# Attention's products in halves of 64 rows, two side by side, with the low part of a pair made one pair later

## The reference

```python
# layer 0: x = x + out_proj(layernorm(selective scans of conv(in_proj(layernorm(x)))) * silu(z))
# layer 1, with O = 96 and N = 4096 positions an image
g_x, theta_x, phi_x = (_conv1x1(x, w, b).reshape(B, O, N) for w, b in ...)
f1 = jnp.einsum('bon,bom->bnm', theta_x, phi_x)
f_div_C = jax.nn.softmax(f1, axis=-1)
y = jnp.einsum('bnm,bom->bon', f_div_C, g_x)
return _conv1x1(y, W_w, W_b) + x
```

## Time and profile before

| what | value |
|---|---|
| median of 3 runs | 9250.66 us (9244.29 to 9259.2) |
| profiled execution | 9256.15 us |
| its span, first to last instruction | 9254.4 us |
| mean granted TensorE clock | 0.981 |
| busy: TensorE, VectorE, ScalarE, GpSimd | 93%, 80%, 66%, 36% |

### The profile page before, as it was taken

One profiled execution on the slowest core, in us unless ns is written; L12 is line 12 of the kernel. 1 busy time (PEld: TensorE's weight loads), 2 busy tenths in 40 slices (PEclk: granted clock), 3 DMA queues, 4 the chain that ended last, 5 costly groups with the idle time before them and its releaser, 6 DMA issues. The chain is left out here.

```text
span 9254.4 us, 103902 instructions
## 1 busy us (share of the span) xinstructions
PE 8642.6 (93%) x26448; PEld 4648.4 (50%) x26448; DVE 7377.0 (80%) x8229; ACT 6091.9 (66%) x7440; POOL 3295.4 (36%) x1853
## 2 busy tenths in 40 slices
PE   7899998999989998899988999889998899988999
PEld 3336743367433674336733367333673336733476
DVE  6987779877798777987679876798767987689876
ACT  6765677656776567765677556775567755677566
POOL 2870028600286002860038600385003850038400
PEclk9999999999999999999999999999999999999999
DMA  1320013200132001320013200232002320023200
GB/s 53 111 87 13 10 56 112 80 13 10 57 111 82 11 11 59 115 76 10 11 63 111 76 10 11 65 116 71 8 12 68 111 73 8 11 72 114 66 8 12
DMA packets 286693, 503.21 MB, mean 54 GB/s; under 512 B 142155, under 2 KB 143215, under 8 KB 253431
## 3 DMA queue, kind: packets, MB, share of 16 engines
q1 hardware_dynamic: 286199, 497.81, 17.9%
HBM read 467.99 MB, written 29.47 MB: 54 GB/s over the span
## 5 line engine op out<-in xcount | busy, mean ns | idle before, releaser
L1400 DVE TENSOR_TENSOR pl<-pf,ph 128x1024 fp32r<-128x1024 f32 x1024 | 1254.3, 1225 | 1007.1 <-ACT ph L1020 999.5
L1253 DVE TENSOR_TENSOR_SCAN h<-ps,h,dbu 128x512 f32<-128x512 f32 x1536 | 1884.2, 1267 | 59.8 <-POOL dbu L1087 29.9
L1087 POOL TENSOR_TENSOR dbu<-bs,du 128x1024 f32<-128x1024 f32 x768 | 1808.1, 2369 | 54.1 <-POOL du L1078 54.1
L1020 ACT ACTIVATE ph<-pf 128x1024 fp32r<-128x1024 f32 x1024 | 1085.3, 1060 | 750.3 <-PE ps L708 750.0
L885 ACT ACTIVATE ps<-dt,negA 128x512 f32<-128x512 f32 x1536 | 1037.5, 687 | 684.8 <-DVE h L1253 684.8
L1014 ACT ACTIVATE pf<-ps 128x1024 f32<-128x1024 f32 x1024 | 1050.4, 1026 | 530.7 <-PE ps L695 513.3
L1066 POOL MEMSET pad<- 128x66 f32 (+1 forms) x64 | 7.2, 200 | 3853.2 <-DVE fa L1429 3853.0
L1384 DVE TENSOR_REDUCE mx<-ps 128x1 f32<-128x512 f32 x1792 | 1168.6, 683 | 78.8 <-PE ps L606 62.5
L1261 DVE TENSOR_TENSOR hc<-h,ps 128x1024 f32<-128x1024 f32 x768 | 937.9, 1221 | 110.3 <-PE ps L487 19.7
L487 PE MATMUL ps<-xhl,selr 128*128 128x512 f32 x1536 | 768.1, 585 | 238.8 <-DVE hc L1261 238.6
L1072 POOL TENSOR_TENSOR dt<-dt,ze 128x1024 f32<-128x1024 f32 x256 | 604.0, 2359 | 1061.3 <-ACT dt L878 1061.3
(11 more groups left out here) (204 smaller groups left out, 14540.6 us busy)
## 6 DMA issues: line engine op xcount, KB each, us to landing
bs<-rows SPq DMA_DIRECT2D x256, 1024.0 KB, 5.1
bs<-rows SPq DMA_DIRECT2D x512, 256.0 KB, 6.1
xa<-in_x SPq DMA_DIRECT2D x130, 256.0 KB, 2.9
xb<-in_x SPq DMA_DIRECT2D x130, 128.0 KB, 3.0
out<-fa SPq DMA_DIRECT2D x64, 256.0 KB, 2.1
rdb<-rden SPq DMA_DIRECT2D x56, 192.0 KB, 3.4
out<-fa SPq DMA_DIRECT2D x64, 128.0 KB, 2.4
xhl<-ct SPq DMA_DIRECT2D x256, 8.0 KB
```

Of the source, the lines that this page charges most:

```text
L1020: A(ph[:, mp % 2, :, :], pf[:, mp % 2, :, :], ACT.Copy).then_inc(S["ph_ready"], 1)
L1087: pool.tensor_tensor(dbu[:, q, :, :], bs[par][:, q, :, :], du[:, r:r + 1, :].to_broadcast([P, 2, T]), ALU.mult).then_inc(S["dbu_ready"], 1)
L1253: dve.tensor_tensor_scan(h[:, j, ::step], ps[:, 2 + e, ::step], dbu[:, q, e, ::step], h[:, j, end:end + 1], ALU.mult, ALU.add)\
L1400: TT(pl[:, mp % 2, :, :], pf[:, mp % 2, :, :], ph[:, mp % 2, :, :].bitcast(F32), ALU.subtract)\
```

## The change

Every fp32r product of attention is cut into halves over rows 0 to 63 and 64 to 127 of the array, issued in turn, so that neighbours in the queue use different halves and different banks. The 96 channels of scores, three times, and the shift row are laid out anew over 64 + 64 + 64 + 64 + 33 rows for each of a pair's blocks, in `th1`, `thx`, `thy` for the queries and `ph1`, `ph2`, `ph3` for the keys. `scores_1` makes three halves for either block and `scores_2` two more. `weigh` gathers the upper halves in bank 5, so the old sum now is two banks that are read and added (`read_sum` on both ScalarE and VectorE). A block of maxima is a lower half ahead of three pairs of halves and an upper half behind them, in one bank (6 or 7). `TOPS`, `WY_AT` and `WR_AT` move. VectorE makes the low part of a pair in the next pair's turn, between its second and third block. The low part of theta is made in four pieces, the high part gets a second copy, and phi's rows are copied to their other places in the mixing steps. The shift goes to two rows with one DMA each. The diff, cut (where code of `top`, `scores` and `weigh` is removed, it is that above):

```diff
-        thc = [[sb(f"thc{q}{i}", [O + 1, T], F32R, where=vx) for i in range(2)] for q in range(2)]
+        th1 = [sb(f"th1{q}", [P, T], F32R, where=vx) for q in range(2)]
+        thx = [sb(f"thx{q}", [P, T], F32R, where=vx) for q in range(2)]
+        thy = [sb("thy0", [P, T], F32R, where=vx)]
         mx = sb("mx", [P, 4, NU // 4], where=vx)
...
-        TOPS = [0] + [2] * 4 + [3] * 8 + [0] * 3
+        TOPS = [0] * 2 + [2] + [3] * 10 + [0] * 3
         FIRST_TOP = [sum(TOPS[:m]) for m in range(MP)]
         assert sum(TOPS) == NU
         LAG = 2
-        DEN_AT, RB_AT, WY_AT, WR_AT = 5, 8, 10, 12
+        DEN_AT, RB_AT, WY_AT, WR_AT = 5, 8, 13, 15
+        LOW, UP = slice(0, R), slice(R, P)
...
                         sp.wait_ge(S["nmx_ready"], i + 2)
-                        for t in range(4):
-                            sp.dma_start(thc[1 - par][0][O:O + 1, t * P:(t + 1) * P].bitcast(F32), nmr[:, t:t + 1].bitcast(F32))\
-                                .then_inc(S["shift_loaded"], 16)
+                        for row in (thx[1 - par][LO:LO + 1, :], thy[1 - par][O:O + 1, :]):
+                            sp.dma_start(row.bitcast(F32).rearrange("o (p j) -> o p j", j=4), nmr[:, :].bitcast(F32)).then_inc(S["shift_loaded"], 16)
...
-                def top(j, i, par, t, m, bank):
...
+                def top(j, i, c, par, rows):
+                    n = b * (NU * (NCH - 1)) + c * NU + (j + 1)
+                    t, m = j // (NU // 4), j % (NU // 4)
+                    if rows == LOW:
+                        if j == 0:
+                            pe.wait_ge(S["thh_ready"], i + 1)
+                            pe.wait_ge(S["thl_ready"], i * 4 + 1)
+                        pe.wait_ge(S["top_read"], i * NU + (j + 1))
+                    else:
+                        pe.wait_ge(S["top_half"], n)
+                    q = mm(ps[:, 6 + j % 2, :], th1[par][rows, :].rearrange("p (k t) -> p t k", t=4)[:, t, :], ph1[rows, m * T:(m + 1) * T],
+                           start=(rows == LOW), stop=(rows == UP))
+                    q.then_inc(S["top_half" if rows == LOW else "top_ready"], 1)
...
-                def scores(mp, c, i, par, first):
+                def scores_1(mp, c, i, par, first, j=None):
                     s = i * MP + mp
...
+                    if mp == 0 and not first:
+                        pe.wait_ge(S["thl_ready"], i * 4 + 4)
+                        pe.wait_ge(S["thx_ready"], i + 1)
+                        pe.wait_ge(S["shift_loaded"], b * (32 * (NCH - 1)) + (c * 32 + 32))
+                    pe.wait_ge(S["pf_ready"], s + 1)
+                    bank = 2 * (mp % 2)
+                    one, other = slice(2 * mp * P, (2 * mp + 1) * P), slice((2 * mp + 1) * P, (2 * mp + 2) * P)
+                    t1, tx = th1[par], thx[par]
+                    def low(n):
+                        if n < 2:
+                            return mm(ps[:, bank, :], (ph1, ph2)[n][LOW, one], t1[LOW, :], start=(n == 0), stop=False)
+                        return scores_0(mp, par, 0)
+                    def up(n):
+                        if n < 2:
+                            return mm(ps[:, bank + 1, :], (ph1, ph2)[n][UP, other], (t1, tx)[n][UP, :], start=(n == 0), stop=False)
+                        return scores_0(mp, par, 1)
+                    if j is not None:
+                        top(j, i + 1, c, 1 - par, LOW)
+                    for n in range(2 if mp == 0 and first else 3):
+                        if j is None:
+                            low(n)
+                            q = up(n)
+                        else:
+                            up(n)
+                            q = low(n)
+                    q.then_inc(S["s1_done"], 1)
+                    if j is not None:
+                        top(j, i + 1, c, 1 - par, UP)
+                def scores_0(mp, par, e, stop=False):
+                    rows = (slice(0, LO + 1), slice(R, O + 1))[e]
+                    return mm(ps[:, 2 * (mp % 2) + e, :], ph3[rows, mp * P:(mp + 1) * P], (thx, thy)[e][par][rows, :], start=False, stop=stop)
+                def scores_2(mp, i, par, first):
+                    pe.wait_ge(S["s1_done"], i * MP + (mp + 1))
+                    bank = 2 * (mp % 2)
+                    one, other = slice(2 * mp * P, (2 * mp + 1) * P), slice((2 * mp + 1) * P, (2 * mp + 2) * P)
+                    t1, tx = th1[par], thx[par]
                     early = mp == 0 and first
...
+                    mm(ps[:, bank, :], ph1[UP, one], t1[UP, :], start=False, stop=False)
+                    mm(ps[:, bank + 1, :], ph1[LOW, other], t1[LOW, :], start=False, stop=False)
+                    mm(ps[:, bank, :], ph2[UP, one], tx[UP, :], start=False, stop=not early)
+                    q = mm(ps[:, bank + 1, :], ph2[LOW, other], t1[LOW, :], start=False, stop=not early)
                     if early:
...
+                        q.then_inc(S["s2_done"], 1)
                         shift(i)
+                        pe.wait_ge(S["s2_done"], b + 1)
                         pe.wait_ge(S["thc_ready"], b + 1)
...
+                        scores_0(mp, par, 0, True)
+                        q = scores_0(mp, par, 1, True)
                     q.then_inc(S["st_ready"], 1)
-                def weigh(mp, i):
+                def weigh(mp, e, i, c, par=0, j=None):
                     s = i * MP + mp
...
+                    if e == 0:
+                        pe.wait_ge(S["pl_ready"], s + 3)
+                        if mp == 0:
+                            pe.wait_ge(S["sum4_read"], i + 1)
+                            pe.wait_ge(S["sum5_read"], i + 1)
+                    m = 2 * mp + e
+                    def half(n, bank, rows):
+                        g, p = ((gth, ph), (gtl, ph), (gth, pl))[n]
+                        return mm(ps[0:O + 1, bank, :], g[rows, m, :], p[rows, mp % 2, e, :],
+                                  start=(m == 0 and n == 0), stop=(m == MT - 1 and n == 2))
+                    if j is not None:
+                        top(j, i + 1, c, 1 - par, LOW)
+                    for n in range(3):
+                        if j is None:
+                            half(n, 4, LOW)
+                            q = half(n, 5, UP)
+                        else:
+                            half(n, 5, UP)
+                            q = half(n, 4, LOW)
+                    if e == 1:
+                        q.then_inc(S["pv_ready"], 1)
+                    if j is not None:
+                        top(j, i + 1, c, 1 - par, UP)
...
-                        scores(mp, c, i, par, not before)
+                        blocks = list(range(FIRST_TOP[mp], FIRST_TOP[mp] + TOPS[mp])) if nxt else []
+                        third = blocks.pop(0) if len(blocks) == 3 else None
+                        blocks += [None] * (2 - len(blocks))
+                        scores_1(mp, c, i, par, not before, third)
+                        if mp >= LAG:
+                            weigh(mp - LAG, 0, i, c, par, blocks[0])
+                        elif before:
+                            weigh(mp - LAG + MP, 0, i - 1, c)
+                        scores_2(mp, i, par, not before)
                         if mp == 0 and nxt:
                             theta(c + 1, i + 1, before)
-                        blocks = range(FIRST_TOP[mp], FIRST_TOP[mp] + TOPS[mp]) if nxt else ()
-                        for j in blocks[:2]:
-                            top(j, i + 1, 1 - par, j // (NU // 4), j % (NU // 4), 5 + j % 2)
                         if mp >= LAG:
-                            weigh(mp - LAG, i)
+                            weigh(mp - LAG, 1, i, c, par, blocks[1])
                         elif before:
-                            weigh(mp - LAG + MP, i - 1)
-                        for j in blocks[2:]:
-                            top(j, i + 1, 1 - par, j // (NU // 4), j % (NU // 4), 5 + j % 2)
+                            weigh(mp - LAG + MP, 1, i - 1, c)
                         if before:
                             if mp == WY_AT:
                                 if nxt:
                                     pe.wait_ge(S["thf_ready"], i + 2)
+                                    pe.wait_ge(S["top_read"], (i + 1) * NU + (NU + 2))
                                 output(i - 1, 0)
                             if mp == WR_AT:
                                 output(i - 1, 1)
...
-                    A(thc[par][0][0:O, :], thf[:, :], ACT.Copy).then_inc(S["thh_ready"], 1)
+                    A(th1[par][0:O, :], thf[:, :], ACT.Copy).then_inc(S["thh_ready"], 1)
+                    A(thx[par][R:O, :], thf[R:O, :], ACT.Copy).then_inc(S["thx_ready"], 1)
...
+                        A(ph1[O:P, bass.ds(c * T, T)], phf[R:O, :], ACT.Copy)
+                        A(ph2[O:P, bass.ds(c * T, T)], phf[LO:R, :], ACT.Copy)
+                        blocks = phf[0:LO, :].rearrange("p (a e k) -> p a e k", e=2, k=P)
+                        for e in range(2):
```

(42 more changed lines are left out.)

86 lines of the change are left out of this document (31 added, 55 removed).

## The result

After the change the kernel takes 9994.22 us, median of 4 runs (9989.01 to 10002.31), beside 9251.92 for the kernel before on the same chip: 1.0799 times as long [1.0786, 1.0812], 742 us more. Predicted were 9815, or 562 more, and a range of 9480 to 10300. The direction and the places were right, the size was 180 us short.

The account below looks back on a forecast made before the run. TensorE was taken as the bound (busy 56.53 of 56.70 us in an attention chunk). Middle chunks + 542, first + 29, last - 9 us: 9256 + 562 = 9818, the median 5 lower, predicted 9815; range 9480 to 10300.

Parts of the forecast that it names:

- The slot and the saving of 3.7 us: TensorE in attention: two halves side by side take one 0.234 us slot, saving one slot a pair, 3.7 us a chunk.
- (a): Rival: halves not side by side, slot 0.47, near 12,100; milder form, load waits for row group, near 10,650; 10% together.
- (b): Rival: halves only partly side by side, slot 0.28 to 0.30, three-block pairs 4.1 us, near 10,250; chance 10%.
- The head's wait: Head of chunks 2 to 7: TensorE stands still 4.9 us for shift DMAs queued behind the stores, 48 times.
- The loop: Three-block pairs: maxima and low part between TensorE and VectorE take 3.8 us against 3.28 of slots, 4.8 us a chunk.
- The chunk's start: Start of a middle chunk: waits for the old sum, 2.0, and pair 1's low part, 1.1; net 2.8 us.
- I take 2.5 us a chunk: Attention: half clock after TensorE's waits of 4.9 and 2.0 us costs 2.5 us a chunk, bounds 0 and 4.
- What a middle chunk has more: Sum for a middle chunk: - 3.7 + 4.9 + 4.8 + 2.8 + 2.5 = + 11.3 us, 48 times.
- The first chunk: First chunk of an image, no head wait or old sum: - 3.7 + 4.8 + 2.5 = + 3.6 us, 8 times.
- Outside the loops: Mixing steps: four more ScalarE copies lie ahead of ScalarE's 3.63 us wait for VectorE and cost nothing.
- (c): Rival: only the head's wait is real, loop quicker and clock unharmed, + 2.7 us a middle chunk, near 9,350; chance 7%.
- (d): Rival: faster, TensorE's slots set every chunk, head wait under 3 us and no loop, 9,020; chance 5%.

Follow-up runs that it names:

- e1: Kernel after the change, with the shift row's two DMAs issued before the two stores of the finished chunk: 9650.32 us, ratio 1.0431.
- e3: Kernel after the change, with the upper half of each block of maxima issued one slot earlier: 10008.09 us, ratio 1.0825.
- e4: Kernel after the change, with a weighing's six halves issued as three upper ones, then three lower ones: 10000.16 us, one profiled run.
- e5: Kernel after the change, with VectorE's low part cut in two, one piece before and one behind the third block: 10234.83 us, ratio 1.1048.
- e9: Kernel after the change, with TensorE's wait for the low part moved down to the products that read it, low part whole: 9844.45 us, ratio 1.0642.
- e8: Kernel after the change, with the low part cut in two and TensorE's wait for it moved to the products that read it: 9864.86 us, ratio 1.0661.
- e2: Kernel after the change, with 20 products that nobody reads put ahead of the head's wait for the shift row: 9930.89 us, ratio 1.0737.
- e10: Kernel after the change, with e1 and e8 joined, the old sum's copy earlier and theta's second copy later on ScalarE: 9452.91 us, ratio 1.0215.
- e12: e10 plus theta's last three low pieces in pairs 13 to 15, low part between all three blocks, maxima over 12 pairs, output product from pair 14: 9341.61 us.
- e6: Kernel after the change, with each block of maxima as one product over all 128 rows instead of two halves: 10474.74 us, ratio 1.1311.

## Why the prediction was right, and where it was short

- **The slot and the saving of 3.7 us: right.** Products over different halves of the rows start 0.01 us apart, and the next two 0.23 later; a pair without maxima takes 2.56. Rivals (a) and (b) fall with these rows. (The sum of (a) also leaves out the head's wait that it says stays; with it (a) would have been near 12,350.) So does the load rule that (a) drew on: the Trainium skill ("TensorE: Matmul & The Clock Gate", Part 3) lets a load run beside a product only where the row group differs, and here L736's load (917.52) runs beside L734's product (917.52), and both are of the upper rows. The load of a block's weights, read with a step, takes 307 ns instead of 190 and lies beside other work.
- **The head's wait: right.** 4.9 predicted, 5.0 where the loop does not turn. e1 takes it away and shows the order of SyncE's queue as its cause.
- **The loop: right in size (3.81 against 3.84), wrong in one link.** Not three slots but the semaphore between the halves keeps the upper half back (e3; in e4 the distance is 0.68 as well). And beside the chain through C there is a second one, which e5 uncovered: B behind TensorE's wait for the low part. e5 shortened the first and drew out the second, e9 loosened only the second, and neither shortened a round; e8 did both and it fell to 3.53.
- **The chunk's start: right, and its clock too.** 2.04 for the sum (2.0 predicted), 1.10 for pair 1's low part (1.1). "I take 2.5 us a chunk" for the clock is what the chunks of e2 without a fall give. That it is exact is luck: it was picked between bounds of 0 and 4, not summed from rows, and the second fall comes in only 15 of 40 chunks.
- **What a middle chunk has more.** 13.6 measured, 11.3 predicted. Of the 2.3, 0.1 is the head's wait, 0.6 the turn of the loop, and 1.6 stand in chunks without any fall of the clock (62.25 in e1, which has no wait at the head, against 56.8 before: 5.5, where the sum has - 3.7 + 4.8 + 2.8 = 3.9). Of the 1.6, 0.5 are there when the low part of pair 1 ends (14.8 after the first score in e1, 14.3 in the sum), and 0.3 are nine rounds at 3.84. Some 0.4 are the output products: the pair of the last chunk with the first of them is 1.25 longer than its neighbours (3.81 against 2.56), before it was 0.86 (3.64 against 2.78). These pairs hold a change between full and half products, which the prediction took as nothing, some 1 us a chunk at most. The rest, 0.4, I can't place.
- **The first chunk: near in size, by another cause.** 3.6 predicted, 4.3 measured. The sum gives it 2.5 for the clock, though neither of the two waits that were to bring the clock down is in it. What it has are TensorE's waits for the low parts of pairs 0 and 1, and e9, which puts that wait later, takes 3.7 of the 4.3 away.
- **Outside the loops: wrong.** "They cost nothing" holds for the copies in 7 of the 8 mixing steps of an image, whose cover was read from the earlier trace rows. In the first step there is another chain behind them, theta's, and 57 us were lost there. I had read the cover in one step and used it for all.
- **The sum of the misses.** 2.3 x 6 = 13.6 us an image in the middle chunks, 0.7 in the first, 7.1 in the first mixing step, 0.4 less in the last chunk: 21 of the 180 / 8 = 22.5. The other 1.5 I can't place.
- **Rivals (c) and (d).** (c), only the head's wait, is refuted by the loop's rounds of 3.84. (d), faster, needed the head's wait under 3 us and no loop. e10 to e12 have the first at every head (at the loop's turns TensorE still idles 1.4 to 2.1), but the loop is then VectorE's own work (3.53 in e8, against 3.28 of slots). In e12 the first mixing step is still 19.4 us in the mean of the images, 6.9 more than before, 55 us in all. The distance between stores over a turn is 59.4 where it is 57.3 elsewhere: 2.1 x 16 = 34 us. The middle chunks away from a turn are 0.5 longer than before, 24 us over 48. Against this the last chunks are 34 us shorter (40.2 each against 44.5). These are the large parts of the 80 us that e12 is slower, not all of them. No run took the mixing step's wait or the turn away.

## What to carry to other kernels

When a step moves later on one engine, follow what stands behind it in every queue: three pairs' delay of the output cost 344 us here, through two DMAs that stood behind two stores. In a loop between two engines look for every chain through it before shortening one, and put a wait at the instruction that reads the data, not at the head of its group. A cover read in one step of a stage holds only for steps with the same work behind it: look at the first and the last of them too. And when the body of a loop grows, look at the place where it turns back: the mean of many rounds hides it. Before a chunk is taken as typical, compare it with the others of its kind; here the clock fell once in some and twice in others.

## What was not expected of the hardware

- The two row halves of TensorE go through their own products independently: a product of the lower rows started 0.08 us before one of the upper rows that stood ahead of it in the queue (e4), with no loss of time. In the kernel after an upper product starts 0.15 us before a lower one that stood ahead of it.
- Going from half to full products and back left the loads idle for 0.36 and 0.24 us at full clock (e6), and cost 481 us over the kernel.
- Weights of 64 x 128 values read with a step of four values load in 0.31 us at full clock, those of the scores beside them in 0.18 (L736's at 917.52).
- A wait of TensorE of 5.03 us was followed by some 6 us at 1.2 GHz. A later wait of 2.0 us stands in all 48 middle chunks, and in the 40 that were looked at one by one the clock fell to 0.50 behind it in 15 and stayed at 1.00 in 25. Chunks with this second fall took 71.5 us, those without 68.9 (heads without a turn of the loop), and 1.2 of these 2.6 were there before it, when theta was read.
- Where the loop over two chunks turns back, TensorE idled 1.4 to 1.9 us with no releaser in e1, 16 times, with two packets of instructions of some 16 KB around that head. The kernel before, with 26448 products instead of 38480, has no such idle time, and no such packet over four middle chunks (890 to 1145).
